# Value products of an attention loop in blocks of 32 queries, turned by VectorE's block transpose instead of TensorE's

## What is computed

```python
score1 = einsum('bhqd,bhkd->bhqk', qh, kh)
s2 = einsum('bhqd,qkd->qbhk', qh, rel_k)          # relative keys
attn = softmax((score1 + s2) / sqrt(D), axis=-1)
w1 = einsum('bhqk,bhkd->bhqd', attn, vh)          # value product
w2 = einsum('qnk,qkd->qnd', se, rel_v)            # relative value product
out = (w1 + w2).transpose(0, 2, 1, 3).reshape(B, T, E)
return out @ Wo.T + bo
```

## Time and profile before

| | |
|---|---|
| Runs of the kernel before | 754.75, 756.34, 756.58 us; median 756.34 |
| Profiled execution | 756.94 us, span 755.1 us |
| Attention loop in the span | from about 229 to 417 us |
| Granted TensorE clock, mean over the span | 0.888 |

### The profile page before, as it was taken

How to read it: one execution, slowest core, us unless ns; L and a number is a source line. 1 busy time by engine, 2 the same in 40 slices (tenths; PEclk the granted TensorE clock), 3 DMA queues, 4 the chain that set the end, 5 groups by cost and what they waited for, 6 DMA issues and landing times. The chain is left out here.

```text
span 755.1 us, 26992 instructions
## 1 busy us (share of the span) xinstructions
PE 577.0 (76%) x10048; PEld 442.5 (59%) x10048; DVE 428.5 (57%) x1998; ACT 402.4 (53%) x1129; POOL 394.1 (52%) x436
## 2 busy tenths in 40 slices
PE   3888888888679989999999666776403999999900
PEld 1655565565556666667767433333203999999900
DVE  1666666666357678777785423645631555555517
ACT  4666666666205555555556243444203999999800
POOL 3454454455148688888886101656660555555510
PEclk9999999999979999999999785756555999999955
DMA  6365565565756666676653027111121222222238
GB/s 238 131 232 200 205 230 191 189 231 189 251 145 193 183 186 195 178 195 193 197 170 115 1 69 229 48 42 45 44 74 36 68 70 68 70 70 70 57 106 235
DMA packets 124140, 106.41 MB, mean 141 GB/s; under 512 B 9216, under 2 KB 100864, under 8 KB 123776
## 3 DMA queue, kind: packets, MB, share of 16 engines
q1 hardware_dynamic: 115456, 93.88, 40.0%
q0 software_dynamic: 4352, 8.95, 3.6%
q10 hardware_dynamic: 4224, 2.10, 0.9%
HBM read 57.15 MB, written 45.65 MB: 136 GB/s over the span
## 5 line engine op out<-in xcount | busy, mean ns | idle before, releaser
L473 POOL TENSOR_TENSOR sc<-sc,mx 128x1024 f32<-128x1024 f32 x64 | 121.3, 1897 | 55.6 <-DVE mx L613 55.6
L383 POOL TENSOR_SCALAR QD<-q_all,mask 128x128 f32<-128x128 f32 x128 | 89.5, 712 | 98.3 <-DVE pre L348 95.0
L613 DVE CUSTOM_DVE_ANT_0 sc<-banks,s2t 128x128 f32<-128x128 f32 x512 | 113.0, 286 | 47.1 <-PE banks L523 46.8
L1173 POOL DMA_INDIRECT expert_outputs<-yr,xr x72 | 72.1, 1001 | 80.0 <-DVE yr L1210 75.2
L662 ACT ACTIVATE PT<-banks 128x512 f32<-128x512 f32 x128 | 69.7, 595 | 76.6 <-PE banks L538 76.3
L940 POOL DMA_INDIRECT expert_inputs<-rows,slotu x64 | 61.9, 967 | 52.5 <-DMA expert_inputs<-rows,slotu 19.6
L339 DVE COPY s2stage<-banks 128x512 f32<-128x512 f32 (+1 forms) x90 | 76.6, 852 | 16.5 <-PE banks L248 16.5
L1144 ACT ACTIVATE hid<-banks,w1b 128x128 f32<-128x128 f32 x288 | 82.3, 369 | 4.2 <-PE banks L1113 4.2
L248 PE MATMUL banks<-RK,QD 32*128 32x128 f32 x1024 | 78.5, 454 | 4.0 <-DVE s2stage L339 0.9
L1113 PE MATMUL banks<-xt,w1b 128*128 128x128 f32 x576 | 77.8, 279 | 0.0
L1130 PE MATMUL banks<-w2b,hid 128*128 128x128 f32 x576 | 76.4, 276 | 0.3 <-ACT hid L1144 0.3
(11 more groups left out here) (121 smaller groups left out, 1001.5 us busy)
## 6 DMA issues: line engine op xcount, KB each, us to landing
s_scratch<-s2stage SPq DMA_DIRECT2D x32, 1024.0 KB, 4.9
s2t<-s_scratch SPq DMA_DIRECT2D x64, 512.0 KB, 4.6
xr<-expert_inputs SPq DMA_DIRECT2D x72, 64.5 KB, 1.8
xz<-in_xz SPq DMA_DIRECT2D x8, 512.0 KB, 5.9
yb<-expert_outputs SPq DMA_DIRECT2D x16, 256.0 KB, 4.8
KB<-k_all SPq DMA_DIRECT2D x32, 64.0 KB, 3.4
q_all<-in_xT SPq DMA_DIRECT2D x1, 2048.0 KB, 9.0
w1a<-in_w1T SPq DMA_DIRECT2D x1, 2048.0 KB, 8.8
```

What stands on the lines that cost most here:

```text
L383: op = pool.tensor_scalar(QD[G % 3][:, :, h, :], q_all[:, :, quad(G)].rearrange("p b t -> p t b"), mask[:, h:h + 1], None, ALU.mult)
L473: pool.tensor_tensor(sc[U % RING][:], sc[U % RING][:], mx[U % RING][:].unsqueeze(2).broadcast_to([P, HH, T]), ALU.subtract)\
L613: op = dve.tensor_tensor_reduce(out=sc[r][:, h, :], in0=ps[2 * (U % 2) + h // 4][:, h % 4 * T:(h % 4 + 1) * T], in1=s2t[r][:, h, :], scale ...
L1173: pool.indirect_dma_start(yg_dram, bass.IndirectOffsetOnAxis(xr[k][:, D:].bitcast(U32), 0), yr[k][:], None).then_inc(s_ys[k], 16)
```

## The change

value_product takes the queries in four blocks of 32. For each head it makes four products, one a block, in the four column groups, with the same weights; the result of head h stands in columns 32 h to 32 h + 31 of bank 6, block j on partitions 32 j on. ScalarE's copy into w1e is as it was. turn_values moves from TensorE to VectorE: one block transpose (32x32 blocks) of w1e into a new tile wt, after which a query's 9 numbers of a head lie side by side; VectorE takes the reciprocals. The normalising product moves from VectorE to GpSimd, which multiplies in place in wt, ahead of its addition into TOT. normalise_values and the two wn buffers go; wt is single. The relative product at even s waits on the copy of bank 7 by ScalarE (s_e7) instead of on s_wn.

```diff
--- before.py
+++ after.py
@@ -411,7 +411,7 @@
             w1e = sb4("w1e", [P, BANK])
             w2e = sb4("w2e", [P, GBH, QL])
             w2q = [sb4(f"w2q{i}", [P, H, 32]) for i in range(2)]
-            wn = [sb4(f"wn{i}", [P, H, DH]) for i in range(2)]
+            wt = sb4("wt", [P, H, QL])
             rec = sb4("rec", [P, B * H])
 
             s_xb = sem("inputs_loaded_again")
@@ -477,9 +477,13 @@
                     def add_value(b):
                         if b == 0:
                             pool.wait_ge(s_tot, 2)
+                        turned = wt[:, :, 0:DH]
+                        pool.wait_ge(s_rec, b + 1)
+                        pool.tensor_tensor(turned, turned, rec[:, b * H:(b + 1) * H].unsqueeze(2)
+                                           .broadcast_to([P, H, DH]), ALU.mult).then_inc(s_wn, 1)
                         pool.wait_ge(s_wn, b + 1)
                         pool.wait_ge(s_acc2, pieces_before(2 * b + 4))
-                        pool.tensor_tensor(TOT[:, b], TOT[:, b], wn[b % 2][:], ALU.add).then_inc(s_acc1, 1)
+                        pool.tensor_tensor(TOT[:, b], TOT[:, b], wt[:, :, 0:DH], ALU.add).then_inc(s_acc1, 1)
 
                     def add_relative(n, values):
                         to = TOT[:, n % 2 * H:(n % 2 + 1) * H, n // 2, :]
@@ -546,11 +550,11 @@
                             pe.wait_ge(s_e6, bank6_jobs(S))
                         pe.wait_ge(s_exp, 2 * S)
                         for h in range(H):
-                            i, j = h // QJ, h % QJ
                             bh = b % GB * H + h
-                            mm = pe.matmul(ps[6][32 * j:32 * j + DH + 1, i * T:(i + 1) * T], V9[:, b, h, :],
-                                           PT[b // GB % 2][:, bh // 2, 0:T // 2, bh % 2, :], start=True, stop=True,
-                                           tile_position=(0, 32 * j))
+                            for j in range(QJ):
+                                mm = pe.matmul(ps[6][32 * j:32 * j + DH + 1, h * QL:(h + 1) * QL], V9[:, b, h, :],
+                                               PT[b // GB % 2][:, bh // 2, j * QL // 2:(j + 1) * QL // 2, bh % 2, :],
+                                               start=True, stop=True, tile_position=(0, 32 * j))
                         mm.then_inc(s_w1, 1)
 
                     def relative_product(g, k, bank):
@@ -561,15 +565,6 @@
                                                relv[:, T - 1 - q, :], PT[g % 2][:, :, q // 2, :, q % 2],
                                                start=True, stop=True, tile_position=(0, 32 * j))
                         mm.then_inc(s_w2, 1)
-
-                    def turn_values(b):
-                        pe.wait_ge(s_e6, w1_copied(b))
-                        if b:
-                            pe.wait_ge(s_wn, b)
-                            pe.wait_ge(s_e7, relative_jobs(2 * b + 3, 0))
-                        for i in range(4):
-                            mm = pe.transpose(ps[7][:, i * T:(i + 1) * T], w1e[:, i * T:(i + 1) * T], ident[:])
-                        mm.then_inc(s_w1t, 1)
 
                     content_scores(0)
                     for g in range(VG // 2, VG):
@@ -583,21 +578,17 @@
                             content_scores((S + LEAD) // 2)
                         if S < NU:
                             turn_scores(S)
-                        if S >= 3 and S % 2:
-                            turn_values((S - 3) // 2)
                         if S >= 2 and S % 2 == 0:
                             value_product((S - 2) // 2)
                         if 1 <= g < NG and s < 4:
                             if s % 2:
                                 pe.wait_ge(s_e6, bank6_jobs(S))
-                            else:
-                                pe.wait_ge(s_wn, (S - 2) // 2)
+                            elif g > 1 or s:
+                                pe.wait_ge(s_e7, 2 * (g - 1) + s // 2)
                             relative_product(g - 1, s, 6 if s % 2 else 7)
                     pe.wait_ge(s_add, NU)
                     for k in range(JOBS):
                         relative_product(NG - 1, k, k)
-                        if k == 0:
-                            turn_values(B - 1)
 
                 @block.vector
                 def _(dve):
@@ -616,16 +607,13 @@
                                                           op1=ALU.max, accum_out=mx[r][:, h:h + 1])
                         op.then_inc(s_add, 1)
 
-                    def normalise_values(b):
-                        turned = ps[7][:].rearrange("p (h r) -> p h r", r=32)
-                        at = rec[:, b * H:(b + 1) * H].unsqueeze(2)
+                    def turn_values(b):
+                        dve.wait_ge(s_e6, w1_copied(b))
+                        if b:
+                            dve.wait_ge(s_acc1, b)
+                        dve.transpose(wt[:].rearrange("p h r -> p (h r)"), w1e[:]).then_inc(s_w1t, 1)
                         dve.wait_ge(s_w1t, b + 1)
-                        dve.reciprocal(at, turned[:, :, DH:DH + 1]).then_inc(s_rec, 1)
-                        dve.wait_ge(s_rec, b + 1)
-                        if b >= 2:
-                            dve.wait_ge(s_acc1, b - 1)
-                        dve.tensor_tensor(wn[b % 2][:], turned[:, :, 0:DH], at.broadcast_to([P, H, DH]), ALU.mult)\
-                            .then_inc(s_wn, 1)
+                        dve.reciprocal(rec[:, b * H:(b + 1) * H].unsqueeze(2), wt[:, :, DH:DH + 1]).then_inc(s_rec, 1)
 
                     def turn_relative(n):
                         if n >= 2:
@@ -640,7 +628,7 @@
                             copy_values(dve, g, 4 + g % 2)
                     for S in range(NU + 3):
                         if S >= 4 and S % 2 == 0:
-                            normalise_values((S - 4) // 2)
+                            turn_values((S - 4) // 2)
                         if S + LEAD < NU:
                             scores(S + LEAD)
                         for n in range(pieces_before(S), pieces_before(S + 1)):
```

## The result

The changed kernel takes 834.41 us (833.06 to 839.64, 4 runs) against 755.92 us for the kernel before (754.75 to 756.58, 4 runs): 1.105 times, with a 95% interval of 1.100 to 1.111. Forecast were 797 us and a range of 764 to 826.

The account below looks back on a forecast made before the run. Instruction packets were taken to bound TensorE in the attention loop: +36.5 us over seven groups, +2.0 first group, +2.1 tail, in all +40.6 on 756.94, so 797.5, put at 797 as median; range 764 to 826.

Parts of the forecast that it names:

- the array's own work hardly changes: TensorE in the attention loop: value product +0.1 us a batch, transposes gone; its own work falls 0.4 us a pair.
- the ring through VectorE: Attention loop: content scores, sums, reciprocal and product, sums, next content scores; 5.05 us a pair, +0.5 by the change.
- GpSimd stays under: Attention loop: GpSimd's added product costs 1.6 us a group, 21.5 busy in all, under the group's length.
- The rival of a longer ring: Attention loop: packets hidden, only VectorE's added 0.5 us counts; 760 to 773 us, chance 0.13.
- The rival of a floor for small products: Value product: 32-column products follow no faster than 16 ns, +1.1 us a batch; 810 to 826 us, chance 0.07.
- the term 6.8 x 4.3 = 29.2 us a group: Attention loop: 6.8 instruction packets a group at 4.3 us each, against 23.98 us now; +36.5 us over seven groups.
- 24.3: Attention loop: us a group without the packets, summed from its four pairs of steps; +0.3 on today's group.
- a loaded hole: Attention loop: TensorE's stop of 1.05 us ending at 250.57, score loads running; read as 5.3 us a packet.
- the idle tail: After the loop, no other transfer running: two TensorE stops on issue 256 instructions apart, read as 3.45 us a packet.
- its case of 3.45 (24.8): Attention loop: packets at 3.45 us take 23.5 a group, under the ring; dense stretches add 0.5; 766 us in all.
- packets near 5.3 throughout: Attention loop: every packet takes about 5.3 us, the total lies above 826 us; chance 0.03.

Follow-up runs that it names:

- move_only: Changed kernel with the value product as before (16 products of 128 queries), against the kernel before on the same chip: 811.92 us, 1.002 times.
- after_pairs: Changed kernel with two heads packed into each value product, 32 products a batch instead of 64: 771.37 us, 1.022 times the kernel before.

## Why the prediction was wrong, and where it was right

**Right.** That instruction packets cost the time, that the array's own work hardly changes, that the ring through VectorE grows by 0.3 to 0.5 us a group and costs nothing beside the packets, that GpSimd stays under: the counts (96 packets), the holes at packet ends and nowhere else, the value product's 1.04 us, the transposes' 0.69 (13.8 / 20), the loss with the split alone and its absence with the move alone. The rival of a longer ring is what move_only is, 1.002. The rival of a floor for small products falls with the 1.04 us and with after_pairs, and so does the Trainium skill's 25 ns from start to start ("TensorE: Matmul & The Clock Gate", the section on 56 ns): 128 products in 1.04 us are 8 ns each in four column groups. The same skill's sentence that crossing a block of instructions is mostly hidden ("Runtime: NRT & Kernel Launch", Instruction fetch mechanics) is not borne out either: with 96 blocks instead of 73 holes of up to 4.16 us stand in the loop.

**The step that failed** is the term 6.8 x 4.3 = 29.2 us a group, with the larger of it and 24.3 taken as the group. Measured are 35.0; over seven groups (35.0 - 23.98) x 7 = 77 us instead of 36.5, and that difference of 40 us covers the error of 37 (797 against 834). Three things were wrong in it.

One price for all packets. The term lets all 6.8 packets of a group pass at the packets' own pace. TensorE waited for 15 of 34. The others took 5.1 us each by its own work and other waits, and what it could have done faster there was not saved up, since only one packet is held ahead: in this stretch of none of the twelve traces does a packet's transfer start more than 0.8 us before the first instruction of the packet in front of it. A group is then the sum, packet by packet, of the longer of the two, which is more than the longer of the two sums. The split without loads (15 packets of 3.3 us and 20 of 4.7 make its 142 us) shows this error alone: at 3.3 us a packet the term would give 6.9 x 3.3 = 22.8, and the group the 24.0 of the kernel before; measured are 28.5. The prediction allowed 0.5 us a group for it in its case of 3.45 (24.8).

The time of a packet under load. 5.3 us was read from a loaded hole and 3.45 from the idle tail, and I took 4.3, arguing that a slower loop spreads its loads. The packets that the changed kernel waited for took 5.3 us. The value for the loop was the one that the loop's own row showed. I gave "packets near 5.3 throughout" 0.03.

The clock. The sum kept TensorE at the 2.4 GHz level and had no term for it. The changed kernel was granted 0.88 on average, and products at 1.2 GHz lengthen the busy time by 3.0 us a group, 21 us over seven groups. That the lower level comes with the holes is shown: every one of its ten stretches begins in a hole or just behind one, and the kernel before, with 0.5 us of waits on issue in five groups, has none. That holes alone bring it is not: without loads of scores TensorE waited 20.2 us in five groups of the split kernel, 15 times and up to 2.2 us, and kept 1.00. How much of the 3.0 us would come back if the clock alone stayed up isn't shown either, since a TensorE that is faster between holes also reaches the next one sooner.

The three overlap, and no run separates them in the changed kernel: what each has of the 5.8 us a group between 29.2 and 35.0 is open. Open too is what the time before a packet's transfer starts consists of, 0.8 and 1.7 us on quiet transfer engines and 1.7 and 2.6 beside loads: no run changed the packets themselves.

## What to carry to other kernels

Count an engine's instructions as a cost of their own: 256 of them are a packet, the packets that TensorE waited for took 3.3 and 4.3 us on quiet transfer engines and 4.3 and 5.3 beside the loads, and a stretch of the list that issues 256 in less time has to stop. Price it packet by packet and not by the average over a loop, because a slow packet gives next to nothing to the dense one behind it. Cutting matmuls into smaller ones at equal columns cost the array 0.1 us a batch here, and by its instructions nearly all of the 78 us; packing two heads into one product, columns wasted and all, took back four fifths of the loss. When a resource is forecast to be short, price it by rows of the same stretch, and ask what its holes do to the clock.

## What the runs showed of the hardware

TensorE's holes stand a multiple of 256 instructions of its list apart, 109 of 109 in twelve traces. A packet that it waits for comes in three steps: the transfer starts 0.8 and 1.7 us (split alone, changed kernel) after the packet before it was entered, 1.7 and 2.6 beside loads of scores at a DMA share of 0.47, takes 1.1 to 1.25, and its first instruction starts 1.4 us after the transfer's end, loads or none. And the price is not only the hole: behind one of 2.33 us TensorE ran a stretch of 3.4 us at 0.51 of its clock, while a hole of 2.7 us elsewhere, and 15 holes of up to 2.2 us in the split kernel without loads, left it at 1.00. The 1.04 us of 128 small products, 8 ns each in four column groups, was the other surprise.
